# A forward row transform on TensorE whose moving table has 40 columns in place of 128

## What is computed

```python
def _spectral_conv(x, w):
    x_ft = jnp.fft.rfft2(x, norm='ortho')
    out = jnp.einsum('bixy,ioxy->boxy', x_ft[:, :, :M1, :M2], w.astype(x_ft.dtype))   # M1 = M2 = 20
    ...
    return jnp.fft.irfft2(out_ft, s=(H, W), norm='ortho')

for sw, cw, cb in ((sw0, cw0, cb0), (sw1, cw1, cb1), (sw2, cw2, cb2), (sw3, cw3, cb3)):
    x1 = _spectral_conv(x, sw)
    x2 = jnp.einsum('bchw,oc->bohw', x, cw) + cb[None, :, None, None]
    x = _gelu(x1 + x2)
```

## Time and profile before

| | us |
|---|---|
| median of 3 runs | 1254.29 |
| lowest and highest of them | 1248.22, 1260.06 |
| the profiled execution, its own time | 1258.07 |
| its span, first to last instruction | 1256.2 |

### The profile page before, as it was taken

The page is one execution under the profiler, slowest core; times in us unless marked ns, Lnnn a source line. Parts: engine busy times, 40 slices in busy tenths (PEclk is TensorE's granted clock), DMA queues, the critical chain, the costliest instruction groups (busy, mean ns, idle before and its releaser), DMA issues.

```text
span 1256.2 us, 34589 instructions
## 1 busy us (share of the span) xinstructions
PE 1124.3 (90%) x15996; PEld 743.5 (59%) x15996; DVE 641.5 (51%) x872; ACT 406.2 (32%) x554; POOL 114.0 (9%) x108
## 2 busy tenths in 40 slices
PE   5899899989989998998998999899568998489996
PEld 4578577767757436775776777571135887433332
DVE  2358237535823223582384466332442576876776
ACT  2232232223123672322322232237424775310000
POOL 5000000000000000000000000000011644150111
PEclk9999899999989998999999999999756999579998
DMA  5320220030024003102201300200200000000000
GB/s 169 103 55 2 83 76 2 22 120 19 2 91 134 4 10 112 44 2 91 68 2 52 106 3 7 99 2 5 55 1 0 2 2 2 1 1 1 6 5 9
DMA packets 24614, 49.26 MB, mean 39 GB/s; under 512 B 9805, under 2 KB 10856, under 8 KB 23829
## 3 DMA queue, kind: packets, MB, share of 16 engines
q1 hardware_dynamic: 21972, 45.97, 11.7%
q10 hardware_dynamic: 2066, 0.80, 0.3%
q0 software_dynamic: 432, 0.29, 0.1%
HBM read 32.87 MB, written 13.51 MB: 37 GB/s over the span
## 4 chain that ended last, share of the span: by engine, by line
PE 76%; DVE 12%; DMA 4%; ACT 3%; issue 2%; SPq 1%; POOL 1%; POOLq 0%; ACTq 0%; DVEq 0%
PE PSALL L1103 21%; PE PSALL L961 8%; PE PSALL L1071 7%; PE PSALL L978 6%; PE PSALL L450 5%; DVE WORK L1295 4%; PE PSALL L1094 4%; PE PSALL L1181 4%; PE PSALL L1046 3%; PE PSALL L439 3%; PE PSALL L375 3%; PE PSALL L1191 2%; PE PSALL L440 2%; DMA spec_scr<-MIXED 2%; DVE WORK L1314 1%
## 5 line engine op out<-in xcount | busy, mean ns | idle before, releaser
L1314 DVE STREAM_TRANSPOSE WORK<-PSALL 128x1024 f32<-128x1024 f32 x128 | 152.4, 1229 | 340.2 <-PE PSALL L1071 340.2
L1103 PEld LDWEIGHTS PSALL<-EW,WORK 64*128 64x128 f32 x4096 | 256.4, 197 | 65.1 <-issue 48.7
L1103 PE MATMUL PSALL<-EW,WORK 64*128 64x128 f32 x4096 | 272.7, 288 | 12.4 <-DVE WORK L1314 12.4
L1231 ACT ACTIVATE X<-PSALL,TABLES 128x1024 f32<-128x1024 f32 x128 | 141.7, 1114 | 356.6 <-PE PSALL L1103 356.6
L1295 DVE STREAM_TRANSPOSE WORK<-PSALL 128x1024 f32<-128x1024 f32 x100 | 119.1, 1230 | 58.5 <-PE PSALL L961 54.7
L978 PE MATMUL PSALL<-TABLES,WORK 128*128 128x128 f32 x1000 | 136.4, 284 | 5.0 <-DVE WORK L1295 0.6
L978 PEld LDWEIGHTS PSALL<-TABLES,WORK 128*128 128x128 f32 x1000 | 118.7, 191 | 32.2 <-issue 18.3
L961 PE MATMUL PSALL<-WORK,DW 32*64 32x256 f32 x3200 | 103.3, 389 | 12.6 <-DMA B<-in_fc_b 12.6
L1291 DVE STREAM_TRANSPOSE WORK<-X 128x1024 f32<-128x1024 f32 x96 | 111.4, 1203 | 0.0
L1212 ACT COPY SPEC<-PSALL 128x400 f32<-128x400 f32 x64 | 53.4, 844 | 175.7 <-PE PSALL L978 172.5
L844 DVE TENSOR_TENSOR WORK<-PSALL,X 128x416 f32<-128x416 f32 x160 | 86.6, 584 | 36.5 <-PE PSALL L440 36.4
(11 more groups left out here) (142 smaller groups left out, 1047.3 us busy)
## 6 DMA issues: line engine op xcount, KB each, us to landing
SW<-in_spec_w SPq DMA_DIRECT2D x160, 80.0 KB, 2.4
spec_scr<-MIXED SPq DMA_DIRECT2D x24, 400.0 KB, 3.2
SPEC<-spec_scr SPq DMA_DIRECT2D x32, 200.0 KB
WORK<-spec_scr SPq DMA_DIRECT2D x16, 200.0 KB
spec_scr<-MIXED SPq DMA_DIRECT2D x32, 80.0 KB, 1.8
WORK<-spec_scr SPq DMA_DIRECT2D x16, 160.0 KB, 2.6
WORK<-in_coords_w SPq DMA_DIRECT2D x2, 1024.0 KB, 4.8
XC<-in_coords_c SPq DMA_DIRECT2D x2, 1024.0 KB, 7.1
```

The source lines that it names most:

```text
L1103: m = pe.matmul(PS[2 * p + z][:, 2 * b * GRID:(2 * b + 2) * GRID], G[64 * z:64 * z + 64, n % 2, b, h:h + 4, :, c].rearrange("p q o -> p (q ...
L1231: nc.scalar.activation(X[:, n].rearrange("p b (z d) c w -> p d z b (c w)", z=2)[:, p, :, :, 2 * t * GRID:2 * (t + 1) * GRID], PSALL[:, 2 * ...
L1314: nc.vector.transpose(G[:, n % 2, 2 * x + y].rearrange("p h o v -> p o h v"), PSALL[:, 4 + 2 * x:6 + 2 * x, :].rearrange("p k (h o v) -> p ...
```

## The change

In `dft_rows` the moving operand is the slice of the table from DH0 to EH0, which has 40 columns, in place of 128 columns from DH0; and the output slice has the same 40 columns. The stationary operand, the number of matmuls, their order, and every wait and signal stay. The five outputs of an image no longer overlap. The 400 columns that ACT reads get the same values.

```diff
             def dft_rows(l, bank, at, z):
                 for kyg in range(KYG):
-
-                    m = pe.matmul(bank[:, at + kyg * KOUT:at + kyg * KOUT + 128],
-                                  z[:, 2 * kyg:2 * kyg + 2].rearrange("p y c v -> p (y c v)"), TABLES[:, l, DH0:DH0 + 128],
+                    m = pe.matmul(bank[:, at + kyg * KOUT:at + (kyg + 1) * KOUT],
+                                  z[:, 2 * kyg:2 * kyg + 2].rearrange("p y c v -> p (y c v)"), TABLES[:, l, DH0:EH0],
                                   start=True, stop=True)
                 return m
```

## The result

The changed kernel takes 1271.25 us (median of 4 runs, 1262.51 to 1273.21; a fifth took 1276.39), the kernel before 1255.11 us (median of 4, 1248.22 to 1260.06). The ratio is 1.013, with a 95% interval of 1.0065 to 1.0194: 16 us slower, where 1275 us was forecast. The profiled execution of the changed kernel took 1262.51 us and is the fastest of it, so its trace shows the mechanism and not quite its usual size. The later executions took 1270.1 to 1276.4 us, with mean granted clocks of 0.922 down to 0.911, against 0.929 in the profiled one.

What follows compares the result with a forecast made beforehand. PE's loop of 4.76 us a round was taken as the bound, DVE close by at 4.63. Clock falls of 4.05 us less tails of 0.61 make 3.4 a layer, 20.6 for six: 1254.3 to 1275 us, range 1248 to 1300.

Steps and rivals of the forecast that it cites:

- The step between instructions: In L978's runs of ten, weight loads keep the step at 0.111 us, so fewer columns save 0 there.
- The rival of the shorter step: In `rows`, the step shortens too, 0.68 us less per image; 17 us for six layers, 1237 us; chance 0.04.
- The tail: The last instruction of a run of ten ends 0.076 us earlier, at eight places a layer: 0.61 us a layer.
- The sign named for the tail: In the groups by line, L978's matmuls must be some 75 ns shorter.
- The clock: In the forward stages and at `mix`, fewer moved columns let TensorE's clock fall to half; net 20.6 us for six layers.
- its thinnest place: End of the forward stage, 236.1 to 241.0 us: L978 streams 1.05 of 4.9 us after, 3.3 before.
- The size of a fall: A 3.4 us fall costs about 1.0 us within the rounds and 1.55 us where `mix` runs.
- The count: Two to three falls within the rounds of a layer and one at its end, 4.05 us a layer before the tails.
- The rival of one fall a layer at the end alone: Falls only at the end of the forward stage, 5.6 us for six layers, 1260 us; chance 0.14.
- The rows it leaned on: Two stretches, 1071.3 to 1078.1 and 928.0 to 951.9 us: PE busy throughout, yet the clock stayed at 0.50.

Runs made afterwards that it cites:

- the kernel with the filler: Changed kernel (width 40) plus an unused 128-column matmul behind each round's second image, 384 columns behind the last image; 1259.48 us, 1.004 to the kernel before.

## Why the prediction was right, step by step

**The step between instructions.** Right. Ten weight loads of L977 take 1.19 us at 40 columns, as at 128, and the round shrank by 0.07 us and not by more. The rival of the shorter step is refuted. By the Trainium skill's table of gaps by columns, "TensorE: Matmul & The Clock Gate", section "Back-to-back issue gap", taken alone, the step would have shortened. The same section calls that the isolated gap and says that in a stream of pairs of weight load and matmul both set the spacing; the trace agrees with that: the step is 0.111 us at 40 columns and at 128.

**The tail.** Right: 0.076 was said, 1.38 - 1.31 = 0.07 us measured, and 4.76 - 4.69 too. Without any fall the stages of the kernel with the filler take 36.30 us at best, against 36.82, so 0.52 a layer where 0.61 was summed. One of the eight places gave nothing: from the first ten of a stage to its `columns` it is 205.59 - 204.21 = 1.38 us before and 208.87 - 207.50 = 1.37 after. The sign named for the tail failed: the single matmul did not get shorter in the profile. Its length is modelled; min, median and max in ns, before and after:

```profile
L978 PE MATMUL PSALL<-TABLES,WORK x1000: 274/275/377, 17.8 to 778.9; 128*128 128x128 f32 x167
...
L977 PE MATMUL PSALL<-TABLES,WORK x1000: 282/283/437, 17.7 to 787.7; 128*128 128x40 f32 x167
```

So a length in the profile can stay while the work behind it shrinks; the step and the end of a run tell.

**The clock.** Right in kind: the falls are in the forward stages and at `mix`, and at the end of the stage, named as its thinnest place. Weight loads in 2.79 of 3.40 us did not hold it up. Columns added between the same loads took most of the falls away, and 64 columns in place of 40 all but one. The Trainium skill, "TensorE: Matmul & The Clock Gate", section "What's actually happening", has the clock gated by default and released by activity; the trace agrees, with 0.50 from 218.7 us on, behind a thin stretch, and 1.00 again from 222.1.

**The size of a fall.** In a round it was put at 1.0 us. The one shown made a round of 4.69 us last from 215.69 to 221.69, DVE's next first transpose, so 6.00 us, and cost 1.3, since it met `columns`:

```profile
221.69 2.38 DVE L1294 STREAM_TRANSPOSE WORK<-PSALL 128x1024 f32<-128x1024 f32 x2 [1.36 <-PE PSALL L961]
```

The mean is the same: 229.7 us less six stages of 36.30 without a fall are 11.9 us for 32.0 at half clock, 1.27 for 3.4. At `mix` 1.55 was said, and 7.72 - 6.16 = 1.56 measured.

**The count.** This was the guess, 2.5 falls in the rounds of a layer and one at its end, and it is the term that was mis-sized. The profiled execution has eight falls of 3.4 us in the rounds, 1.3 a layer, and one at the end in four layers of six, two of them 6.8 us long: 47.7 us at half clock in all. So there were half as many falls in the rounds as said, each dearer than said, and some at the end longer. They cost 11.9 + 7.2 = 19.1 us where 24.3 was said, and less the tails it is 16.0 in place of 20.6. That 1275 came so near to 1271 is in part luck, as these errors partly offset each other. The medians differ by 16.1 us, but the profiled execution is the fastest one, so how the other executions divide their loss is not shown.

The rival of one fall a layer at the end alone was priced at 1260 us, and the kernel with only the last four images narrow, which has its falls only there, takes 1260.79. That is near by chance too: it has falls in four layers of six, three of them 6.8 us long, and only two of the eight tails of a layer are shorter.

**The rows it leaned on.** Two stretches of the tail at half clock, busy all the time, stood for the claim that neither being in flight nor loading weights raises the clock. That was about rising; the changed kernel shows it for falling. But in the first of them, from 928.0 to 951.9, columns moved as well, which the prediction did not count:

```profile
L303 PE MATMUL PSALL<-X,WQKV 64*64 64x260 f32 x12 | 6.7, 662 | 0.0
L320 PE MATMUL PSALL<-WORK,OUTSIDE 65*65 65x256 f32 x12 | 6.7, 662 | 0.0
L306 PE MATMUL PSALL<-X,WQKV 64*64 64x260 f32 x11 | 6.0, 634 | 0.0
L311 PE MATMUL PSALL<-WQKV,X 64*65 64x64 f32 x40 | 5.7, 319 | 0.0
L295 PE MATMUL PSALL<-ident,X 65*64 65x65 f32 x20 | 3.2, 315 | 0.0
```

These are 12912 columns. At 0.87 x 1.84 = 1.60 ns each, an estimate from the prediction's rows, they take 20.7 of the 23.9 us, on 64 or 65 of the array's 128 rows and as many of its columns, and the clock stayed at half. So few moved columns are shown as the cause in the forward stages, where the tiles fill the array; a count of columns alone does not tell what the clock does elsewhere, and why it stays down in the tail is open.

## What to carry to other kernels

Columns that nobody reads are not always waste. Here each matmul loads a full set of weights, the load sets the step, and columns up to its length are nearly free and, in the forward stages, kept TensorE's clock up; cutting them saves only the tail of a run and thins out the stage. Before narrowing, count the columns that move in the thinnest places, not busy time, and put filler where the engine waits anyway, sized to end with the wait.

## What was not expected of the hardware

- Falls differ much in length. The eight in the changed kernel's rounds lasted 3.4 us; one at the start of an inverse stage in the kernel before lasted 10.3 us. Two more matmuls of `keep_busy` a layer, 1.7 us of work that nothing reads, were therefore worth 0.7% of the whole kernel.
- Two executions of the same kernel differ by 1% (1262.5 to 1276.4 us for the changed one) with their mean granted clock (0.929 to 0.911). With one execution of each, this change would have measured as 0.4% and not 1.3%.
- PE in flight for 95% of a stretch and weights loading for 82% of it (3.22 and 2.79 of 3.40 us) were followed by half clock.
